# Two attention layers on one core: another order of the instructions at the end of the first layer

## The reference, cut to what matters

```
layer 1 (L0_xattn), 16 heads of 8 features:
    q = x Wq + bq;  k = ctx Wk + bk;  v = ctx Wv + bv
    out = softmax(q k^T / sqrt(8)) v  Wo + bo
    h   = layernorm(out) * ln_g + ln_b
    out = out + gelu(h W1 + b1) W2 + b2          # 512 hidden features
    x   = x + out
layer 2 (L1_xattn), 16 heads of 64 features:
    x = attention(layernorm(x; g1, b1), itself) Wo1 + bo1 + x
    x = attention(layernorm(x; g2, b2), ctx)    Wo2 + bo2 + x
    a, gate = split(layernorm(x; g3, b3) Wp + bp)
    x = (a * gelu(gate)) Wf + bf + x
```

## Time and profile before

| what | value |
|---|---|
| median of 3 runs | 471.89 us (471.37 to 472.52) |
| the profiled execution's own time | 471.55 us |
| its span | 469.7 us |
| TensorE busy (products) | 450.1 us, 96% of the span |
| VectorE, ScalarE, GpSimd busy | 254.4, 254.9, 215.0 us |
| share of the chain that ended last | PE 84%, DVE 8%, ACT 4%, issue 2%, DMA 1% |
| hardware DMA queue | 8.44 MB, 5.6% of 16 engines' span |

### The profile page before, as it was taken

The page is one execution under the profiler, slowest core; times in us unless marked ns, Lnnn a source line. Parts: engine busy times, 40 slices in busy tenths (PEclk is TensorE's granted clock), DMA queues, the critical chain, the costliest instruction groups (busy, mean ns, idle before and its releaser), DMA issues.

```text
span 469.7 us, 7192 instructions
## 1 busy us (share of the span) xinstructions
PE 450.1 (96%) x2854; PEld 271.5 (58%) x2854; DVE 254.4 (54%) x478; ACT 254.9 (54%) x356; POOL 215.0 (46%) x188
## 2 busy tenths in 40 slices
PE   7988897999999999999999999999999999999896
PEld 4644463566555655655555856545575555754696
DVE  2676635666645473547645566236534546543763
ACT  3854564465667365755545446556517665337633
POOL 5586101046773776644445656754227343245010
PEclk9999999999999999999999999999999999999999
DMA  8500000000000100000001100020000000000001
GB/s 261 192 1 1 1 1 0 1 1 0 1 0 1 34 1 1 0 1 1 1 0 46 33 2 2 1 68 0 1 30 17 2 1 0 2 1 0 1 10 36
DMA packets 7984, 8.89 MB, mean 19 GB/s; under 512 B 560, under 2 KB 6128, under 8 KB 7952
## 3 DMA queue, kind: packets, MB, share of 16 engines
q1 hardware_dynamic: 7952, 8.44, 5.6%
HBM read 7.92 MB, written 0.52 MB: 18 GB/s over the span
## 4 chain that ended last, share of the span: by engine, by line
PE 84%; DVE 8%; ACT 4%; issue 2%; DMA 1%; SPq 0%; DVEq 0%
PE PV L746 17%; PE ST L717 14%; PE ST L637 11%; PE M L688 7%; PE ST L719 5%; PE M L794 5%; PE DEN L761 3%; PE M L702 3%; PE ST L653 2%; PE ST L529 2%; ACT PT L1308 2%; PE M L836 2%; DVE maxw L1509 1%; PE ST L355 1%; PE ST L677 1%
## 5 line engine op out<-in xcount | busy, mean ns | idle before, releaser
L1146 POOL TENSOR_TENSOR psums<-PT 128x1024 f32<-128x1024 f32 (+1 forms) x32 | 76.2, 2380 | 141.3 <-ACT PT L1308 141.1
L1308 ACT ACTIVATE PT<-ST 128x1024 f32<-128x1024 f32 (+1 forms) x96 | 98.1, 1025 | 38.3 <-PE ST L719 37.1
L717 PE MATMUL ST<-R 64*128 64x512 f32 (+1 forms) x576 | 105.1, 406 | 0.0
L1650 DVE TENSOR_REDUCE maxw<-M 128x1 f32<-128x512 f32 x128 | 83.6, 688 | 37.1 <-PE M L688 36.8
L746 PE MATMUL PV<-PT,V 128*64 128x512 f32 (+1 forms) x384 | 89.5, 601 | 0.0
L1150 POOL TENSOR_TENSOR psums<-psums,PT 128x1024 f32<-128x1024 f32 x32 | 76.0, 2375 | 2.5
L688 PE MATMUL M<-R 64*128 64x512 f32 (+1 forms) x256 | 71.6, 363 | 1.2 <-DVE maxw L1652 0.4
L717 PEld LDWEIGHTS ST<-R 64*128 64x128 f32 (+1 forms) x576 | 57.4, 171 | 14.7 <-ACT PT L1308 8.3
L688 PEld LDWEIGHTS M<-R 64*128 64x128 f32 x256 | 36.9, 184 | 37.4 <-issue 28.4
L746 PEld LDWEIGHTS PV<-PT,V 128*64 128x64 f32 (+1 forms) x384 | 24.7, 136 | 53.1 <-issue 52.6
L1316 ACT ACTIVATE AT<-PV 128x512 f32<-128x512 f32 x32 | 19.1, 598 | 58.6 <-PE PV L746 58.5
(11 more groups left out here) (247 smaller groups left out, 681.4 us busy)
## 6 DMA issues: line engine op xcount, KB each, us to landing
Wo<-in_wo SPq DMA_DIRECT2D x2, 512.0 KB, 6.3
xnT<-in_xT SPq DMA_DIRECT2D x2, 256.0 KB, 3.2
psums<-in_sel SPq DMA_DIRECT2D x1, 512.0 KB, 4.5
X<-in_x SPq DMA_DIRECT2D x1, 512.0 KB, 6.1
w<-in_w SPq DMA_DIRECT2D x2, 256.0 KB, 6.6
PT<-in_wq SPq DMA_DIRECT2D x1, 512.0 KB, 7.4
PT<-in_wk SPq DMA_DIRECT2D x1, 512.0 KB, 7.6
PT<-in_wv SPq DMA_DIRECT2D x1, 512.0 KB, 8.0
```

Of the source, the lines that this page charges most:

```text
L717: return pe.matmul(u[0:ph.KC, h, :], R[head(h), g % 3, part_k, 1, k], R[head(h), g % 3, part_q, 0, :], start=(n == 0), stop=False)
L1146: ins = pool.tensor_tensor(s, p[:, 0], p[:, 1], ALU.add)
L1308: act.activation(PT1[0:ph.KC, g % 2, c], bank(("st", g, c))[0:ph.KC, :, :], ACT.Exp, scale=HD ** -0.5).then_inc(ph.exp, 1)
L1650: ins = dve.tensor_reduce(maxw[:, g % 2, c, HD * h:HD * h + 1], m[:, :], AX, ALU.max, negate=True)
```

## The change

The end of layer 1 gets another order on TensorE, ScalarE and VectorE. Batch 0's last values (`weigh0(3, ...)`, `turn0(4)`) and its chain come earlier, batch 1's tiles 5 to 7 later, tiles 6 and 7 mostly inside `start_attention`. Batch 0's chain works in the bank DEN instead of taking banks of the ring. Seven products of `hold` are gone. In the loop over tiles each set of maxima comes one slot earlier. `project` is cut into a leading part (products with `xh`) and a trailing part (with `xl`). `scale_features` writes `xh` first, and `hidden` signals after each product. V0all and the loaded `wq0`, `wk0`, `wv0` lie elsewhere in V, so that layer 2's first values can be written while V0all is still read.

The diff, cut (the ScalarE and VectorE lists show all calls that changed):

```diff
-        V0all = Vflat[:, 0:1280]
+        V0all = Vflat[:, 6912:8192]
...
+        apart = {("b0", 0), ("o", 0, 0), ("t", 0, 0), ("t", 1, 0)}
...
+            if key in apart:
+                return DEN[:, :]
...
                 if n == 6 and c == 0:
                     pe.wait_ge(w2_read, 1)
+                    pe.wait_ge(xn_done[1], 1)
+                    pe.wait_ge(full_done1[0], 1)
...
def hidden(b):
-                        ins = pe.matmul(u[:, mm, :], w1[:, m * P:(m + 1) * P], xnT[...], start=True, stop=True)
-                    ins.then_inc(w1_done, 1)
+                        pe.matmul(u[:, mm, :], w1[:, m * P:(m + 1) * P], xnT[...],
+                                  start=True, stop=True).then_inc(w1_done, 1)
                     if n == 0:
+                        maxima0(6, 2, 3)
+                    if n == 1:
                         maxima0(6, 4, 5)
-                    if n == 1:
-                        maxima0(6, 6, 7)
-                        weigh0(5, 1)
+                        scores0(5, 0)
...
def second(b):
-                        if b == 0 and 4 * t + m in (7, 9, 11, 13):
-                            k = 4 * t + m - 7
-                            if k == 0:
-                                pe.wait_ge(cp0_done, 3)
-                            hold(1, PV)
-                            maxima0(7, k, k + 1)
                     if b == 0 and t == 0:
+                        maxima0(6, 6, 7)
+                        scores0(5, 1)
+                    if b == 0 and t == 2:
                         turn0(6)
-                    if b == 0 and t == 1:
-                        scores0(6, 0, 1)
...
TensorE, the loop over n and what follows:
             for n in range(TB):
+                maxima0(n + 1, 1)
                 if n > 0:
                     weigh0(n - 1, 0)
...
                 scores0(n, 0, 1)
-                maxima0(n + 1, 1)
+                maxima0(n + 1, 2)
...
                 scores0(n, 2)
-                maxima0(n + 1, 2)
+                maxima0(n + 1, 3)
                 scores0(n, 3)
-                maxima0(n + 1, 3)
+                if n < TB - 1:
+                    maxima0(n + 2, 0)
                 scores0(n, 4)
                 if n < TB - 1:
-                    maxima0(n + 2, 0)
-                turn0(n + 1)
+                    turn0(n + 1)
             to_queries0(0, 0)
+            weigh0(3, 0)
             maxima0(5, 0, 1)
-            weigh0(3, 0)
+            weigh0(3, 1)
+            turn0(4)
+            to_queries0(0, 1)
+            scores0(4, 0)
             maxima0(5, 2, 3)
-            weigh0(3, 1)
-            scores0(4, 0)
-            maxima0(5, 4, 5)
-            to_queries0(0, 1)
-            hold(1, DEN)
             back0(0)
             scores0(4, 1)
+            maxima0(5, 4, 5)
+            scores0(4, 2)
+            out0(0)
             maxima0(5, 6, 7)
-            out0(0)
-            scores0(4, 2)
+            weigh0(4, 0)
+            weigh0(4, 1)
             turn0(5)
-            weigh0(4, 0)
-            hold(2, DEN)
-            scores0(5, 0, 1)
             maxima0(6, 0, 1)
-            weigh0(4, 1)
-            turn(0, 0, False)
-            maxima0(6, 2, 3)
-            weigh0(5, 0)
-            scores0(5, 2)
+            turn(0, 0)
             hidden(0)
             second(0)
-            turn0(7)
-            scores0(6, 2)
-            weigh0(6, 0)
-            scores0(7, 0)
-            weigh0(6, 1)
-            scores0(7, 1)
-            turn(1, 0, False)
-            weigh0(7, 0)
-            scores0(7, 2)
+            scores0(5, 2)
+            weigh0(5, 0)
+            maxima0(7, 0, 1)
+            weigh0(5, 1)
+            scores0(6, 0)
+            maxima0(7, 2, 3)
+            scores0(6, 1)
+            turn(1, 0)
...
             def start_attention():
-                project(0)
+                project_leading(0)
+                maxima0(7, 4, 5)
+                project_trailing(0)
+                maxima0(7, 6, 7)
+                weigh0(6, 0)
+                scores0(6, 2)
+                turn0(7)
+                scores_max(0, 0)
+                values(0, 0)
+                scores0(7, 0)
+                weigh0(6, 1)
+                scores_max(0, 1)
+                scores0(7, 1)
+                values(0, 1)
+                weigh0(7, 0)
+                scores0(7, 2)
+                scores_max(0, 2)
+                project(1)
+                values(0, 2)
                 weigh0(7, 1)
-                project(1)
-                for c in range(TB):
-                    scores_max(0, c)
-                    values(0, c)
-                    if c in (1, 2):
-                        to_queries0(1, c - 1)
+                scores_max(0, 3)
+                to_queries0(1, 0)
+                values(0, 3)
+                to_queries0(1, 1)
...
ScalarE, the end of layer 1 and the start of attention():
             root(0, 0)
-            exponentials0(5, 0, 1)
             scale_features(0, 0)
-            exponentials0(5, 2)
             gelus(0)
+            exponentials0(5, 0, 1, 2)
+            root(1, 0)
+            exponentials0(6, 0)
+            scale_features(1, 0)
             copy_half0(1, 0)
-            exponentials0(6, 0, 1, 2)
-            root(1, 0)
-            exponentials0(7, 0, 1)
-            scale_features(1, 0)
-            exponentials0(7, 2)
+            exponentials0(6, 1)
...
                 leading(0)
+                exponentials0(6, 2)
+                values(0, 0)
+                exponentials0(7, 0, 1)
+                values(0, 1)
+                exponentials0(7, 2)
+                leading(1)
+                values(0, 2)
                 copy_half0(1, 1)
-                leading(1)
-                for t in range(TB):
-                    values(0, t)
+                values(0, 3)
...
VectorE, the same:
+            normalise0(0, 0)
+            maxima0(5, 0, 1)
             less_maxima0(4)
-            normalise0(0, 0)
-            maxima0(5, 0, 1, 2, 3, 4, 5)
             normalise0(0, 1)
-            maxima0(5, 6, 7)
+            maxima0(5, 2, 3, 4, 5)
             first_out(0)
+            maxima0(5, 6, 7)
+            layernorm(0, O, 0)
             less_maxima0(5)
-            layernorm(0, O, 0)
-            maxima0(6, 0, 1, 2, 3, 4, 5, 6, 7)
+            maxima0(6, 0, 1, 2, 3, 4, 5)
+            maxima0(6, 6, 7)
             less_maxima0(6)
-            maxima0(7, 0, 1, 2, 3, 4, 5, 6, 7)
             second_out(0)
-            less_maxima0(7)
+            maxima0(7, 0, 1)
             layernorm(1, X, 0)
+            maxima0(7, 2, 3)
...
                 trailing_features(1, 0)
+                maxima0(7, 4, 5, 6, 7)
                 trailing(0)
+                less_maxima0(7)
                 maxima(0, 0)
+                maxima(0, 1)
+                maxima(0, 2)
                 trailing(1)
-                for c in range(1, TB):
-                    maxima(0, c)
-                    if c >= 2:
-                        normalise0(1, c - 2)
+                maxima(0, 3)
+                normalise0(1, 0)
+                normalise0(1, 1)
```

More of the change, by code:

```diff
@@ L104, in build @@
         Vflat = V[:, :, :].rearrange("p t n -> p (t n)")
-        V0all = Vflat[:, 0:1280]
+        V0all = Vflat[:, 6912:8192]
         V0last = O.rearrange("p t d -> p (t d)")
         V0cells = V0all.rearrange("p (k u w) -> p k u w", u=4, w=16)
-        wq0 = Vflat[:, 1600:2112].rearrange("p (t n) -> p t n", t=4)
-        wk0 = Vflat[0:C, 2112:2624].rearrange("p (t n) -> p t n", t=4)
-        wv0 = Vflat[0:C, 2624:2752]
+        wq0 = Vflat[:, 5328:5840].rearrange("p (t n) -> p t n", t=4)
+        wk0 = Vflat[0:C, 5840:6352].rearrange("p (t n) -> p t n", t=4)
+        wv0 = Vflat[0:C, 6352:6480]
         maxw0 = maxw[:, :, :, :].rearrange("p b t (a g f) -> p b t a g f", a=2, g=2)
@@ L116, in whole0 @@
             k = n % 3
-            at = 2752 + 2664 * half + 2 * N * k
+            at = 2664 * half + 2 * N * k
             return Vflat[:, at:at + (2 * N if k < 2 else 4 * S)]
@@ L327, in claim_half @@
             def claim_half(key, freed, count, among_maxima):
+                if key in apart:
+                    return half_bank(key)
                 if not among_maxima:
@@ L515, in turn @@
                 pe.wait_ge(xc_done[n], b + 1)
-                u = claim_half(("t", n, b), xn_done[n], b + 1, among_maxima)
+                u = claim_half(("t", n, b), *((xn_done[n], b + 1) if n == 0 else (full_done1[n - 1], b + 1)), among_maxima)
                 for t in range(TB):
@@ L528, in hidden @@
                         m = 2 * (n % 2) + mm
-                        ins = pe.matmul(u[:, mm, :], w1[:, m * P:(m + 1) * P], xnT[:, b * N:(b + 1) * N], start=True, stop=True)
-                    ins.then_inc(w1_done, 1)
+                        pe.matmul(u[:, mm, :], w1[:, m * P:(m + 1) * P], xnT[:, b * N:(b + 1) * N],
+                                  start=True, stop=True).then_inc(w1_done, 1)
```

(54 more changed lines are left out.)

## The result

The changed kernel takes 479.03 us (median of 4 runs, 477.4 to 480.32) against 472.12 us before: ratio 1.0146, 95% interval 1.0123 to 1.0168. It is slower by 1.5%, where 468.5 us and a gain of 0.7% were forecast. The profiled execution took 480.32 us with a span of 478.4.

What follows compares the result with a forecast made beforehand. Before all_scores(0), a chain of short steps hopping between engines bounds it. Holds' 3.7 us less 0.35 of idle gives 3.4 gained: 468.2 for the profiled execution, 468.5 with the median 0.34 higher; range 466.3 to 471.0.

Steps and rivals of the forecast that it cites:

- the clock falls in the new gaps: Rival, gaps at 50.5 to 56.0 us and before 71.0: half clock, 3.0 us a fall; one fall 0.07, two 0.05.
- middle: Stretch from the loop's first turn, turn0(0), to all_scores(0): 20.07 to 95.65 us before, all_scores(0) predicted at 92.3.
- What goes: Between 41 us and all_scores(0): seven holds taken out, 7 x 0.53 = 3.7 us of TensorE time.
- The long waits: TensorE idle 1.14 us before turn0(5), 1.89 before tile 6's maxima, 1.08 before hidden, 1.16 and 1.07 around turn(1,0).
- The sentence on the Trainium skill: Skill passage: frequent small idle gaps between product groups can swing the clock; the prediction said this trace does not agree.
- Loop over batch 0's tiles: First-layer loop: maxima one slot sooner, two waits of 0.16 and 0.19 us a round where 0.16 and 0.34 stood.
- the walk: Step-by-step timing of the four engines' orders: all_scores(0) at 95.65 us before, as in the trace, and 92.3 after.
- hidden to second: Tile 5's exponentials wait behind two table loads, 0.3 and 0.5 us to spare, price nothing; second starts at 61.0.
- second to project: TensorE waits 1.16 us for turn(1,0), then 1.07 for its scaled copy; project begins at 71.0 instead of 80.9.
- Edits costed at nothing: V0all and weight placement, earlier add_bias, claim of turns, project's split: taken as 0; project's bound 0.05 us per call.
- The chance for ScalarE being late: Rival: four places with a long wait each 0.7 us longer, 2.8 of 3.4 us gone, 471.3, no change; chance 0.10.

Runs made afterwards that it cites:

- experiments 1: Changed kernel with 11 holds put back in its own long waits: 471.16 us, ratio 0.9984 to the kernel before.
- experiment 2: Kernel before without its seven holds between 41 us and all_scores(0), nothing else: 473.28 us, ratio 1.003.
- experiments 3: Changed kernel with units 2 and 3 of each wide tile's maxima exchanged: 477.89 us, ratio 1.0107 to the kernel before.
- the fourth experiment: Changed kernel with both the 11 holds in its long waits and the exchanged maxima units: 471.63 us, ratio 0.9978 to the kernel before.
- experiment 7: Kernel before with only the changed kernel's loop over batch 0's tiles: 473.55 us, ratio 1.0027.
- experiment 8: Changed kernel with the 11 holds in its long waits and project whole again from its second call on: 471.14 us.
- the ninth experiment: Changed kernel with holds and exchanged units, 1 hold instead of 2 ahead of turn(1,0) and project, 2 holds in the last stretch: 469.79 us, ratio 0.9961.

## Why the prediction was wrong

The step that failed is the price of the seven holds: the prediction put them down as 3.7 us gained, and the rival that names their use, that the clock falls in the new gaps, at 0.05 for the two falls that came. Measured, the two falls cost 6.4 us before all_scores(0). Two smaller terms were mis-sized as well, the loop and second. By the prediction's own steps, against its middle of 92.3 - 20.07 = 72.2 us and the measured 81.49:

- **What goes** (3.7 us of holds): the count was right, the value wrong. The step took a product that computes nothing as pure cost, to be set against idle time. In both orders these products hold the clock, in the old one in most runs (experiments 1 and 2).
- **The long waits**: right in place and size, each within 0.25 us. The chain VectorE, TensorE, ScalarE was read correctly (for the wait of 0.91 us the view names no releaser).
- **The rival "the clock falls in the new gaps"** is what happened, twice before all_scores(0), at the two places it named. I gave two falls 0.05. The argument against it was that the old stretch keeps 1.00 with its 6.0 us of waits, and that no single wait exceeds 1.89. The old stretch kept it with the help of the holds in question, as experiment 2 shows; without them waits of 0.95 and 1.49 us came before one fall and a single one of 0.37 us before the other, so the longest wait tells little. The total of idle time over 55 us says nothing about 1.7 busy us in 4.5. The price was off too: 3.0 us a fall by the kernel's start; measured 1.7 and 5.2, which is near the 6.0 for two only because one is below and one above.
- The sentence on the Trainium skill ("TensorE: Matmul & The Clock Gate", "A second HAM failure mode: psum-queue depth-cycling") ended with the trace not agreeing. With the changed kernel's trace it agrees: short gaps between groups of products, none above 1.85 us, make the clock swing between its two levels.
- **Loop over batch 0's tiles**: the walk priced maxima next to scores as side by side, since they were so before. It did not ask whether the unit that comes into that place works on free row groups. Exchanging the units gains 1.05 and 1.17 us (experiments 3 and 4); against the old loop the new one loses 0.94 (experiment 7), where the prediction had it gain. The waits of a round were 0.52 us, with 0.16 and 0.19 walked.
- **hidden to second, second to project**: in the prediction second starts at 61.0 and TensorE needs tile 5's exponentials, behind second, at 64.5: 3.5 us. In the changed kernel these are 65.59 and 70.85: 5.26 us, at a clock of 1.00. The walk had second's products at 0.45 us a quarter. Each quarter is 8 instructions and takes 0.8 to 1.06, as in this row of the changed kernel, two quarters in 1.89 us (TensorE's weight loads are shown busy for 1.86 of them):

```profile
67.30 2.05 PE L553 MATMUL DEN<-w,AT 128*128 128x128 f32 x16
69.19 0.60 PE L429 MATMUL M<-ident,maxw 128*128 128x128 f32 x4
```

  What is left between the prediction and the fourth experiment, 73.89 - 72.2 = 1.7 us, arises mainly there: with both counted from turn0(0), tile 6's maxima start 0.25 us later than walked, turn(1,0) behind second 1.9 us later. No run tested it by itself. The walk of the kernel before gave 95.65 all the same. There the quarters already took 0.9, and TensorE waited for VectorE behind them:

```profile
63.83 1.13 PE L544 MATMUL DEN<-w,AT 128*128 128x128 f32 x8
64.79 0.60 PE L422 MATMUL M<-ident,maxw 128*128 128x128 f32 x4
65.23 1.06 PE L544 MATMUL DEN<-w,AT 128*128 128x128 f32 x8
66.12 0.60 PE L344 MATMUL PV<-work 128*128 128x256 f32 x2
...
75.44 0.50 PE L453 MATMUL ST<-R 28*128 28x512 f32 x2 [0.83 <-DVE R L1524]
```

  That it met the old time was no proof of its terms.
- **Edits costed at nothing**: right for project as far as can be told (experiment 8). The chance for ScalarE being late was not used: ahead of weigh0(5, 0) there is no wait.
- **The sum**: 72.2 + 1.7 (second) + 1.2 (row groups) + 6.4 (clock) = 81.5. It closes by construction, since the terms are the steps from the changed kernel over the first and fourth experiments to the prediction; only the last two were made by edits. In the profiled execution 1.4 more come ahead of turn0(0), which varies by itself, and 1.4 in the rest, where the third fall lies.

## What to carry to other kernels

A product that computes nothing, in front of a wait, may be what keeps TensorE at full clock, as it was here. Before one is removed, list the waits it covers and look at how little TensorE does around them; after a reordering, put such products where the new waits are, and look at the granted clock by windows of a few microseconds before anything else. When products change neighbours, compare their row groups as well as their semaphores. And a walk that reproduces the old time has only been tested on the steps that set it; price each step from its own row.

## What I had not expected of the hardware

- The second fall lasts 13.6 us. In its 12.90 us from 76.50 on TensorE is shown busy for 11.97, through 35 recorded instructions, while the first is over after two products of hidden, 3.4 us. The clock did not come back as soon as the engine had work.
- Behind the same unedited waits of 1.08 and 0.42 us in the last stretch the clock falls in some executions and not in others. Six of ten runs of the fourth kernel were below a mean of 1.000 and some 2 us longer; the profiled one of them fell there.
- At the kernel's start four products of 512 columns took 6.74 us in the changed kernel's profile and 5.68 in that of before, both at half pace for a while (full pace would be 4 x 0.91 = 3.64), with a granted clock of 1.00 shown. In the ninth experiment's profile they took 4.51. Their end, 8.70 us there and 11.58 in the changed kernel, accounts for the shift of the loop's first turn between 18.69 and 21.48 us.
